# The decayed memory read is scaled inside its accumulation bank, and the values are subtracted from there

## The reference

```python
S = S * jnp.exp(b_g)[..., None, None]
kv = jnp.einsum('mbhk,mbhkv->mbhv', k_t, S)
dv = (v_t[None] - kv) * b_beta[..., None]
S = S + k_t[..., :, None] * dv[..., None, :]
o_t = jnp.einsum('mbhk,mbhkv->mbhv', q_t, S)
```

## Time and profile before

| | |
|---|---|
| median of 3 runs | 7432.92 us |
| the profiled execution's own time | 7433.18 us |
| its span, first to last instruction | 7431.5 us |
| mean granted TensorE clock | 0.803 of full |
| DVE busy | 5741.0 us, 77% |
| PE busy | 4567.1 us, 61% |
| POOL busy | 3289.4 us, 44% |
| ACT busy | 3284.2 us, 44% |

### The profile page before, as it was taken

One profiled execution on the slowest core, in us unless ns is written; L12 is line 12 of the kernel. 1 busy time (PEld: TensorE's weight loads), 2 busy tenths in 40 slices (PEclk: granted clock), 3 DMA queues, 4 the chain that ended last, 5 costly groups with the idle time before them and its releaser, 6 DMA issues. The chain is left out here.

```text
span 7431.5 us, 196282 instructions
## 1 busy us (share of the span) xinstructions
PE 4567.1 (61%) x78513; PEld 3915.4 (53%) x78513; DVE 5741.0 (77%) x10216; ACT 3284.2 (44%) x5497; POOL 3289.4 (44%) x2021
## 2 busy tenths in 40 slices
PE   1565656656666666566565666666665656663994
PEld 0455555555555555555555555555555555553662
DVE  5788888888888888888888888888888888883003
ACT  0444445444445444454444544444444445452220
POOL 0545454454454454544545544445445455453003
PEclk9787778877778777787777887777877778876997
DMA  2000000000000000000000000000000000003223
GB/s 80 1 5 5 5 5 5 3 4 5 5 5 5 5 5 5 5 5 2 5 5 5 5 5 5 5 5 5 5 2 5 5 5 5 5 4 108 68 71 99
DMA packets 68598, 107.85 MB, mean 15 GB/s; under 512 B 11824, under 2 KB 57200, under 8 KB 66544
## 3 DMA queue, kind: packets, MB, share of 16 engines
q1 hardware_dynamic: 59248, 69.78, 2.9%
q0 software_dynamic: 8448, 25.18, 1.1%
HBM read 57.32 MB, written 37.62 MB: 13 GB/s over the span
## 5 line engine op out<-in xcount | busy, mean ns | idle before, releaser
L1527 POOL TENSOR_TENSOR state<-state,gc_end 128x512 f32<-128x512 f32 x512 | 594.9, 1174 | 1359.2 <-PE bank L580 1319.0
L574 PE MATMUL bank<-rhs,te 128*64 128x64 f32 x8192 | 451.8, 270 | 887.4 <-DVE rhs L1240 551.3
L574 PEld LDWEIGHTS bank<-rhs,te 128*64 128x64 f32 x8192 | 378.1, 177 | 974.1 <-DVE rhs L1240 925.5
L557 PE MATMUL bank<-state,ke 128*64 128x64 f32 x16384 | 660.3, 249 | 319.3 <-DVE outT L1258 232.2
L557 PEld LDWEIGHTS bank<-state,ke 128*64 128x64 f32 x16384 | 620.9, 161 | 439.9 <-DVE state L1256 247.7
L751 ACT ACTIVATE te<-tt 32x256 f32<-32x256 f32 x1024 | 421.9, 412 | 742.8 <-DVE tt L1224 732.3
L593 PE MATMUL last_two<-dvs,kte 128*64 128x64 f32 x16384 | 638.2, 236 | 180.5 <-DVE dvs L1247 180.5
L1221 DVE TENSOR_TENSOR last_two<-last_two,prod 128x31 f32<-128x31 f32 (+15 forms) x1984 | 692.6, 349 | 68.1
L793 ACT ACTIVATE ke<-kq 32x512 f32<-32x512 f32 x1024 | 642.7, 628 | 201.7 <-DVE kq L1173 188.0
L1219 DVE TENSOR_TENSOR prod<-bd,last_two 128x31 f32<-128x31 f32 (+15 forms) x1984 | 671.1, 338 | 71.9
L593 PEld LDWEIGHTS last_two<-dvs,kte 128*64 128x64 f32 x16384 | 575.3, 149 | 196.7 <-DVE dvs L1247 187.7
(11 more groups left out here) (248 smaller groups left out, 11015.0 us busy)
## 6 DMA issues: line engine op xcount, KB each, us to landing
w_sb<-in_L_ffn_W_dram SPq DMA_DIRECT2D x16, 1024.0 KB, 9.3
expert_rows<-ke SPq DMA_DIRECT2D x1, 8192.0 KB, 21.3
xrows<-expert_rows SPq DMA_DIRECT2D x16, 512.0 KB, 8.3
expert_outputs<-yrow POOLq DMA_DIRECT2D x16, 512.0 KB, 3.4
xt<-_attn_hidden_states_dram SPq DMA_DIRECT2D x32, 128.0 KB, 2.1
xr<-_attn_hidden_states_dram SPq DMA_DIRECT2D x32, 128.0 KB, 2.1
x_after_attention<-xr SPq DMA_DIRECT2D x32, 128.0 KB, 1.7
xo<-x_after_attention SPq DMA_DIRECT2D x32, 128.0 KB, 3.7
```

The lines of the kernel that those rows point to most:

```text
L557: mm = pe.matmul(bank_mem[g][s, q % 4 * DK:q % 4 * DK + DK], ke[:, c, r, q, s], state[:, hh * HQ + q, r, :], start=(r == 0), stop=(r == 1))
L574: pe.matmul(bank_mem[g][s, q % 4 * DK:q % 4 * DK + DK], te[:, q, s], rhs[:, q, :], start=True, stop=True)
L1527: pool.tensor_tensor(sv, sv, gc_end[:, vh, 4 * g:4 * g + 4, c].unsqueeze(2).broadcast_to([P, 4, 2 * DK]), ALU.mult).then_inc(sem(f"state_f ...
```

## The change

Line 1237 writes its product back into the bank it reads from, where it wrote the SBUF tile `rhs`. Line 1240 subtracts what stands in the bank from the values, where it subtracted what stood in `rhs`. The result still goes to `rhs`. So L1237 has one input in PSUM and one in SBUF as before and its output moves from SBUF to PSUM; L1240 had both inputs in SBUF and now has one in PSUM. Both have 128x256 elements in float32, and there are 512 of each. No instruction is added, removed or moved on any engine, and the semaphores that they wait for and raise are the same.

```diff
-                    ln(dve.tensor_tensor(rhs[:, of], ksv, eg_col[:, hh, c, of].unsqueeze(2).broadcast_to([P, 4, DK]), ALU.mult))
+                    ln(dve.tensor_tensor(ksv, ksv, eg_col[:, hh, c, of].unsqueeze(2).broadcast_to([P, 4, DK]), ALU.mult))
                     vv = v_sb[:, c, 2 * g * DK:2 * g * DK + 2 * DK].rearrange("p (h v) -> p h v", h=2).unsqueeze(2).broadcast_to([P, 2, 2, DK])
                     r4 = rhs[:, of].rearrange("p (h g) v -> p h g v", g=2)
-                    vec(dve.tensor_tensor(r4, vv, r4, ALU.subtract), f"rhs_ready{g}", vc + 1)
+                    vec(dve.tensor_tensor(r4, vv, ksv.rearrange("p (h g) v -> p h g v", g=2), ALU.subtract), f"rhs_ready{g}", vc + 1)
```

## The result

The changed kernel takes 7323.74 us (median of 4 runs, 7321.21 to 7325.34) against 7432.8 us before (4 runs): ratio 0.9853, interval 0.9838 to 0.9868. That is 109 us less. 7335 was forecast, with a range of 7305 to 7387. The profiled execution took 7325.34 us, 107.8 us less than the one before.

What follows compares the result with a forecast made beforehand. The attention was taken to run at VectorE's pace plus its waits, with line 518 on TensorE setting line 1205. 7433.2 - 100.8 + 2 = 7334, given as 7335 us, range 7305 to 7387.

Steps and rivals of the forecast that it cites:

- What holds line 1240: Chunk 3's second line 1240: two SBUF inputs beside GpSimd's line 1547 hold it, 1.58 us excess in 63 halves, 99.5 us.
- Line 1240 at 425 ns, line 1237 at +7: VectorE: line 1240 falls to 425 ns, line 1237's bank output costs 7 ns each; together +2 us.
- The longer access to PSUM: VectorE overhead of about 125 ns on PSUM, 60 on SBUF: line 1240 would lose 65 ns each, 33 us, near 7367.
- Line 518's start: TensorE, chunk 3: line 518 starts 0.78 us earlier in one kind of half, 2.0 us in the other.
- Line 518's length, by the clock: TensorE: line 518 takes 2.1 to 2.4 us with the clock back earlier, 3.0 us in the other kind of half.
- The sum: Line 1205 earlier by 1.7 and 1.5 us in the two kinds of half, 3.2 us a pass, 100.8 us altogether.
- the slower rival: TensorE's clock falls in more chunks, 1.6 us each (64 matmuls 1.07 us more at half clock): 7480 or 7530; chance 0.03.
- VectorE's 1.58 us: The excess of the held line 1240 that goes from VectorE in each half with memory steps.
- TensorE's share: How much earlier line 518 ends, which sets line 1205: 1.7 us in one kind of half, 1.5 in the other.
- the 0.78 us of its queue: Rival: TensorE's clock returns no earlier, every half gives only 0.78 us, 49 us in all, 7386; chance 0.13.
- The step that stood on weak ground: VectorE: what comes behind line 1205 follows VectorE's order and moves with it, carrying the 3.2 us a pass.

Runs made afterwards that it cites:

- only_held: Kernel before, with the change made only for the chunk 3, group 1 pair of lines 1237 and 1240; 7322.99 us, ratio 0.9851.
- all_but_held: Kernel before, with the change made for seven of eight instruction pairs, chunk 3, group 1 left as before; 7432.77 us, ratio 1.0.
- output_in_bank: Kernel before, but in chunk 3 line 1240 writes its result into the bank and one more copy takes it to `rhs`; 7487.09 us.
- filler_matmuls: Kernel before, with six small matmuls added in chunk 3 between the first and second group's corrections on TensorE; 7430.39 us, ratio 0.9996.
- rotation_in_bank: Changed kernel, with line 1163 writing the first key rotation product into the update banks and line 1167 reading it there; 7277.72 us, ratio 0.9788.
- work_under_slack: Changed kernel, with two 128x512 scratch clears added on VectorE right behind `right_sides(3)`, ahead of line 1205; 7367.22 us, ratio 0.9911.
- one clear: Changed kernel, with one 128x512 scratch clear on VectorE added in front of `solve` in each half; 7323.96 us, ratio 0.9853.
- before_one_clear: Kernel before, with one 128x512 scratch clear on VectorE added in front of `solve` in each half; 7464.67 us, ratio 1.0043.
- rotation_again: The same kernel as rotation_in_bank, run a second time against the changed kernel; executions of 7321.09 (profiled) and 7280.18 us.

## Why the prediction was right

*What holds line 1240.* Right: its two inputs in SBUF beside GpSimd. only_held and all_but_held show that the 63 instructions are the gain, output_in_bank that an output into SBUF is not needed for the hold.

*Line 1240 at 425 ns, line 1237 at +7.* Measured 421 and +7, as the two lines of `solve` had it. The longer access to PSUM that the Trainium skill gives (Perfetto Trace Analysis, section Optimizing Scalar/DVE Operations) did not show: line 1240 got 4 ns shorter.

*Line 518's start.* 0.78 and 2.0 us earlier were worked out, measured against line 1240's start 0.82 and 1.86.

*Line 518's length, by the clock.* In the half of the earlier trace rows 2.1 to 2.4 us were expected, measured 2.09. In the half of the earlier trace rows the clock fell all the same, as reckoned (3.0 expected, 3.18 measured). But the reason that the prediction gives is not shown. It took from two halves that the clock came back 3.3 to 4.1 us after an unbroken stretch began, and let the closed gap start this stretch earlier. In the changed kernel this holds in the half of the earlier trace rows (back 3.5 us after 3050.22), but not in the half of the earlier trace rows (4.8 us after 2946.48). The filler and the rotation kernels have halves without a gap in which it took 6.5 and 6.3 us and line 518 3.08 and 3.35 us. What the changed kernel does have is a fall of the clock that comes 3.7 us later against line 1240's start, which the prediction did not foresee. So the 2.09 us came within the range, but for a reason that was only argued, and in part by luck. What sets the moment of the fall stays open.

*The sum.* Line 1205's start came 1.9 us earlier in the one kind (1.7 taken) and 1.50 us in the half of the earlier trace rows (1.8 taken). Over its kind the mean is 1.58 us (1.5 taken), and this is luck in part: the prediction mixed 1.8 us with 1.2 us for halves in which the clock is at half when line 1240 starts. Before these were 17 of 31 and they gained 1.6 us; in the changed kernel there are none, the clock is at full there in all 31. A pass was to be 3.2 us shorter, 201.6 us, and is 3.4 us shorter, 201.39. Over 31 passes that is 106 us and not 99, which is 7 of the 9 to 11 us by which the forecast was too high. The term was mis-sized by 0.1 to 0.2 us a half, in the half of the earlier trace rows nearly all of it in line 518's length. The price of the slower rival was low too: 64 matmuls at half clock throughout take 3.66 us (filler_matmuls), 1.58 us more than at full and not 1.07, since the 3.15 us of the earlier trace rows were partly at full clock.

*Was it VectorE's 1.58 us or TensorE's share?* Here they came to nearly the same: 102.9 us off VectorE's busy time, against 63 x 1.58 = 99.5 us expected, and its idle time almost unchanged (-4.9). Had TensorE given only the 0.78 us of its queue, the other half would have become waiting. work_under_slack shows the slack from the other side: of 84.3 us of added work and its gaps 57.8 went under line 1205's wait.

*The step that stood on weak ground* was that all behind line 1205 moves with it. It did in this change, but not in general: the filler's gain in some halves was lost in others, the rotation's was taken back in front of line 1205 in the profiled executions, and one clear cost nothing in one kernel and 32 us in the other.

*What stays open.* Passes of 204.80 us on average were measured in two kernels and of 201.34 to 201.39 us in six profiled executions, though VectorE's busy time differs by 55 us among the latter. The waits for TensorE at half clock make up the difference in the rotation's case. Whether the clock pulls passes to such lengths in general was not settled. Against it, the changed kernel with one clear has the same average, but its passes lie between 200.49 and 202.35 us. The kernel before with one clear had 13 of 30 passes within 0.05 us of 204.80 and the others up to 206.83 in its profile, and 7464 us without the profiler.

## What to carry to other kernels

When a group's mean is well above that of its likes, look at the least, median and greatest duration: a few very long instructions mean that something holds them, and the timeline names it. An instruction of VectorE with both tensors in SBUF can be held for as long as one of GpSimd runs; one input kept in a bank lifts that for a few nanoseconds. Count the gain at the next engine that is waited for. Where that is TensorE, do not count on a closed gap to bring the full clock back: look in several halves at when the clock fell, and give what hangs on it a wide range.

## What the runs showed of the hardware

- A subtraction with both inputs in SBUF was held by GpSimd's instruction (2.00 us against 0.42 us) and ended 0.28 us after it, also when its output went to a bank (1.54 us, ended 0.30 us after it).
- The hold goes both ways: when line 1167 read one input from a bank, it fell from 2393 to 1224 ns and GpSimd's line 1541 from 3217 to 2376 ns.
- A transposition of 128x1024 that began while GpSimd's instruction ran took 1.25 us, as elsewhere.
- A product written into a bank in place took 432 ns for 128x256, into SBUF 425; a subtraction with one input in a bank 421, with none 424 to 426.
- The same 64 matmuls took 2.06 to 2.08 us at full clock and 3.66 us at half. Behind stretches of TensorE without a gap the full clock came back after 3.5 us in one half of the changed kernel, 4.8 us in another, and 6.3 and 6.5 us in halves of two other kernels.
- The executions of a kernel without the profiler can differ from the profiled one by 0.6% (7272 to 7280 against 7321 to 7322 us, rotation_in_bank and rotation_again), the other way in another (7464 to 7465 against 7452 us, before_one_clear), and by under 0.1% in the changed kernel.
